# Mamba's drives: five of sixteen states formed by ScalarE with time on the partitions and turned into PSUM by TensorE

## What is computed

```python
xc = silu(conv(x @ W_in.T, W_conv) + b_conv)          # 256 channels
dt, B, C = split(xc @ W_x.T)                           # ranks 8, 16 and 16
dt = softplus(dt @ W_dt.T + b_dt)
A = -exp(A_log)
# for every time t, channel d, state n of 16:
h = h * exp(dt_t[:, :, None] * A) + (dt_t * xc_t)[:, :, None] * B_t[:, None, :]
y = einsum('bdn,bn->bd', h, C_t)
# y = (y + xc * D) * silu(z), then y @ W_out.T
```

## Time and profile before

| | us |
|---|---|
| median of 3 runs | 3919.7 (3919.11 to 3921.49) |
| the profiled execution, its span | 3921.5 |
| first scan of Mamba to the end of the last | 929.5 |
| from the start of the transformer to the end | 2899.6 |

### The profile page before, as it was taken

The page is one execution under the profiler, slowest core; times in us unless marked ns, Lnnn a source line. Parts: engine busy times, 40 slices in busy tenths (PEclk is TensorE's granted clock), DMA queues, the critical chain, the costliest instruction groups (busy, mean ns, idle before and its releaser), DMA issues.

```text
span 3921.5 us, 110568 instructions
## 1 busy us (share of the span) xinstructions
PE 3707.5 (95%) x43392; PEld 2518.5 (64%) x43392; DVE 3319.6 (85%) x3407; ACT 2915.4 (74%) x6890; POOL 3241.5 (83%) x2370
## 2 busy tenths in 40 slices
PE   7889989988789999999999999999999999999997
PEld 2333333333377777777777777777767777777775
DVE  4999999999688888888888887888878888788885
ACT  7555445553388887888888887888878888888885
POOL 3888888888698888888888888888888888888883
PEclk8999998998899999999999999999999999999999
DMA  1221222212100000000000000000000000000001
GB/s 68 73 76 70 76 71 75 76 71 83 50 16 2 16 3 2 17 2 16 3 6 13 2 16 2 6 13 3 16 2 6 13 2 16 2 6 2 2 3 44
DMA packets 31567, 102.12 MB, mean 26 GB/s; under 512 B 4676, under 2 KB 6600, under 8 KB 30928
## 3 DMA queue, kind: packets, MB, share of 16 engines
q1 hardware_dynamic: 31056, 95.05, 7.0%
HBM read 90.32 MB, written 4.72 MB: 24 GB/s over the span
## 4 chain that ended last, share of the span: by engine, by line
PE 68%; issue 2%; ACT 2%; DVE 0%; POOL 0%; POOLq 0%; ACTq 0%; DVEq 0%
PE ps L1116 17%; PE ps L1043 13%; PE ps L1105 9%; PE ps L1054 8%; PE ps L1093 7%; PE ps L1141 5%; PE ps L1154 3%; PE ps L1078 2%; PE ps L1065 1%; PE ps L1123 1%; PE ps L1129 1%; ACT prob L1246 0%; PE ps L1023 0%; ACT mixed L1255 0%; ACT w_qk L1175 0%
## 5 line engine op out<-in xcount | busy, mean ns | idle before, releaser
L1521 POOL TENSOR_TENSOR resid<-resid,sq 128x1024 f32<-128x1024 f32 x384 | 910.8, 2377 | 3.4 <-DVE sq L1376 2.9
L626 POOL TENSOR_TENSOR read<-state,c_row 128x1024 f32<-128x1024 f32 x256 | 719.8, 2831 | 153.9 <-DVE state L588 84.9
L1543 POOL TENSOR_TENSOR resid<-resid,rnorm 128x1024 f32<-128x1024 f32 x384 | 725.0, 1904 | 18.1 <-POOL rnorm L1535 0.4
L1116 PE MATMUL ps<-mixed,w_vo 128*128 128x128 f32 x6144 | 720.7, 276 | 3.0 <-ACT mixed L1255 2.8
L1116 PEld LDWEIGHTS ps<-mixed,w_vo 128*128 128x128 f32 x6144 | 711.5, 193 | 12.9 <-issue 4.6
L1043 PE MATMUL ps<-w_qk,xs_parts 128*128 128x512 f32 x2304 | 634.6, 411 | 35.4 <-issue 18.1
L1246 ACT ACTIVATE prob<-ps,stat 128x64 f32<-128x64 f32 x3072 | 653.5, 385 | 0.7 <-DVE stat L1396 0.5
L1376 DVE TENSOR_TENSOR sq<-ps,rope_l 128x1024 f32<-128x1024 f32 x384 | 462.4, 1204 | 101.5 <-ACT sq L1208 101.2
L393 PE MATMUL mamba_ps<-read,ident 128*128 128x512 f32 x1024 | 509.6, 638 | 15.4 <-POOL read L626 15.4
L1389 DVE TENSOR_TENSOR resid<-ps,rope_l 128x1024 f32<-128x1024 f32 x384 | 464.3, 1209 | 66.9 <-ACT sq L1208 59.7
L1043 PEld LDWEIGHTS ps<-w_qk,xs_parts 128*128 128x128 f32 x2304 | 412.4, 191 | 148.6 <-issue 73.8
(11 more groups left out here) (138 smaller groups left out, 5676.8 us busy)
## 6 DMA issues: line engine op xcount, KB each, us to landing
c_row<-c_rows SPq DMA_DIRECT2D x128, 512.0 KB, 3.6
w_stage<-w_qk_hbm SPq DMA_DIRECT2D x12, 512.0 KB, 4.7
vo_stage<-w_v_hbm SPq DMA_DIRECT2D x6, 512.0 KB, 3.7
vo_stage<-w_o_hbm SPq DMA_DIRECT2D x6, 512.0 KB, 4.6
xn<-x_hbm SPq DMA_DIRECT2D x4, 512.0 KB, 6.6
kept<-resid SPq DMA_DIRECT2D x8, 256.0 KB, 4.4
resid<-kept SPq DMA_DIRECT2D x8, 256.0 KB, 4.0
out_hbm<-resid SPq DMA_DIRECT2D x8, 256.0 KB, 2.0
```

What stands on the lines that cost most here:

```text
L626: pool.tensor_tensor(read[:, h, g % 2, :], state[:, h, g % 2, :], c_row[:, g % C_AHEAD, :], ALU.mult).then_inc(done[f"rd{h}"], 1)
L1116: last = pe.matmul(bank[:, 0:P], w_vo[:, l % 2, head_at(place_h), :], mixed[:, odd, place_h, :], start=place_h == 0, stop=place_h == HEADS ...
L1521: pool.tensor_tensor(qk[:, tile % 2, cols], qk[:, tile % 2, cols], sq[:, 1 + part, :], ALU.add).then_inc(done[f"rotated{part}"], 1)
L1543: pool.tensor_tensor(heads, heads, norms, ALU.mult).then_inc(done[f"normed{part}"], 1)
```

## The change

For the states 2, 5, 8, 11 and 14 the drive no longer comes from a spread row of B and VectorE. Once for each sequence TensorE turns `dtx` (16 transposes of 128x128, steps "tt0" to "tt3") and B (8 small ones, "tb"), and ScalarE copies them to `dtx_t` and `b_t`, which have time on the partitions. For each of the five states ScalarE scales `dtx_t` by the state's column of `b_t` (eight instructions of 128x256, "td", to `drive_t`), and TensorE turns the result back, eight transposes for each half, into a pair of banks ("p0", "p1"). The scan reads it from there. The step "b" and both drives of these states are gone. `DRIVE_IN_PSUM` shrinks from six states to three, so half 0's drive lies in SBUF for 8 states instead of 10. All order tables are new.

```diff
+DRIVE_IN_PSUM = (4, 10, 15)
+DRIVE_TURNED = (2, 5, 8, 11, 14)
+DRIVE_SPREAD = tuple(n for n in range(D_STATE) if n not in DRIVE_TURNED)
+TURNS_BY_STATE = 4
...
+        if name in ("b", "p0", "p1"):
+            pair = other
+            take(name, k, [2 * pair, 2 * pair + 1], (("sc1" if name == "b" else f"sc{name[1]}", k),))
+            if name == "b" and k % D_STATE in DRIVE_IN_PSUM:
+                take("dr0", k, [2 - 2 * pair, 3 - 2 * pair], (("sc0", k),))
...
+            if g % D_STATE in DRIVE_TURNED:
+                first = SLOTS[f"p{h}", g][0]
+                return ps[:, first:first + 2, :]
...
+                def turn_dtx(q):
+                    def stage(s):
+                        after(pe, ("tx0", s), ("tx1", s))
+                        to = free(f"tt{q}", s)
+                        for j in range(2):
+                            for h in range(HALVES):
+                                first = (2 * q + j) * P
+                                last = pe.transpose(to[:, (2 * j + h) * P:(2 * j + h + 1) * P], dtx[:, s % 2, h, first:first + P],
+                                                    ident[:, :])
...
+                def turn_drive(h):
+                    def stage(g):
+                        after(pe, ("td", g))
+                        free(f"p{h}", g)
+                        to = drive_of(h, g).rearrange("p c n -> p (c n)")
+                        for j in range(SEQ // P):
+                            last = pe.transpose(to[:, j * P:(j + 1) * P], drive_t[:, j, h * P:(h + 1) * P], ident[:, :])
...
+                def take_turned(q):
+                    def stage(s):
+                        after(act, (f"tt{q}", s), ("td", D_STATE * (s - 1) + LAST_TURNED))
+                        act.copy(dtx_t[:, 2 * q:2 * q + 2, :], bank(f"tt{q}", s).rearrange("p (j n) -> p j n", j=2)
...
+                def drive_turned(g):
+                    s, n = divmod(g, D_STATE)
+                    k = DRIVE_TURNED.index(n)
+                    before = D_STATE * s + DRIVE_TURNED[k - 1] if k else D_STATE * (s - 1) + LAST_TURNED
+                    after(act, *[(f"at{q}", s) for q in range(TURNS_BY_STATE)], ("ab", s), ("p0", before), ("p1", before))
+                    for j in range(SEQ // P):
+                        last = act.activation(drive_t[:, j, :], dtx_t[:, j, :], ACT.Identity, scale=b_t[:, s % 2, j, n:n + 1])
...
-                        after(dve, (f"dec{h}", g), (f"dr{h}", g), (f"rd{h}", g - 2))
+                        after(dve, (f"dec{h}", g), (f"p{h}" if g % D_STATE in DRIVE_TURNED else f"dr{h}", g), (f"rd{h}", g - 2))
...
-    nc = bacc.Bacc("TRN2", target_bir_lowering=False, num_devices=1)
+    nc = bacc.Bacc("TRN2", target_bir_lowering=False, num_devices=1, dynamic_dma_scratch_size=1024)
```

More of the change, by code:

```diff
@@ L128, in mamba_slots, with take @@
 def mamba_slots(pe):
-    single = {f"bc{c}": f"abc{c}" for c in range(2)} | {f"o{c}": f"ao{c}" for c in range(2)} | {
-        f"{a}{h}{c}": f"{b}{h}{c}" for a, b in (("x", "ax"), ("z", "az"), ("dt", "relu")) for h in range(HALVES) for c in range(2)}
-    slots, last, turn, pair = {}, [None] * 4, [0, 0], 1
-    def take(name, k, banks, reader):
-        slots[name, k] = banks[0], sorted({last[q] for q in banks if last[q]})
+    single = {f"bc{c}": (f"abc{c}",) for c in range(2)} | {f"o{c}": (f"ao{c}",) for c in range(2)} | {
+        f"{a}{h}{c}": b(h, c) for a, b in (("x", lambda h, c: (f"ax{h}{c}",)), ("z", lambda h, c: (f"az{h}{c}",)),
+                                           ("dt", lambda h, c: (f"abs{h}{c}", f"relu{h}{c}")))
+        for h in range(HALVES) for c in range(2)} | {f"tt{q}": (f"at{q}",) for q in range(TURNS_BY_STATE)} | {"tb": ("ab",)}
+    slots, last, turn, pair = {}, [()] * 4, [0, 0], 1
+    def take(name, k, banks, readers):
+        slots[name, k] = banks[0], sorted({x for q in banks for x in last[q]})
         for q in banks:
-            last[q] = reader
+            last[q] = readers
     for name, k in pe:
         other = 1 - pair
-        if name == "b":
-            pair = k % 2
-            take("b", k, [2 * pair, 2 * pair + 1], ("sc1", k))
-            if k % D_STATE in DRIVE_IN_PSUM:
-                take("dr0", k, [2 - 2 * pair, 3 - 2 * pair], ("sc0", k))
+        if name in ("b", "p0", "p1"):
[3 more added lines that the diff above has]
+                take("dr0", k, [2 - 2 * pair, 3 - 2 * pair], (("sc0", k),))
         elif name in single:
-            take(name, k, [2 * other + turn[other]], (single[name], k))
+            take(name, k, [2 * other + turn[other]], tuple((x, k) for x in single[name]))
             turn[other] ^= 1
@@ L167, in mamba @@
                 (MAMBA_PE, FRONT_PE), (MAMBA_ACT, FRONT_ACT), (MAMBA_DVE, FRONT_DVE), (MAMBA_POOL, FRONT_POOL), (MAMBA_SP, []))]
-        in_sbuf = [g for g in range(2 * BATCH * D_STATE) if g % D_STATE not in DRIVE_IN_PSUM]
+        in_sbuf = [g for g in range(2 * BATCH * D_STATE) if g % D_STATE not in DRIVE_IN_PSUM + DRIVE_TURNED]
         DRIVES, BEFORE = {g: i for i, g in enumerate(in_sbuf)}, dict(zip(in_sbuf[2:], in_sbuf))
@@ L373, in b_rows, with turn_b @@
                     last.then_inc(done["b"], 1)
+                def turn_dtx(q):
[7 more added lines that the diff above has]
+                                                    ident[:, :])
+                        last.then_inc(done[f"tt{q}"], 1)
+                    return stage
+                def turn_b(s):
+                    after(pe, ("abc0", s), ("abc1", s))
+                    to = free("tb", s)
+                    for j in range(SEQ // P):
+                        last = pe.transpose(to[:, j * D_STATE:(j + 1) * D_STATE], x_dbl[0:D_STATE, j * P:(j + 1) * P],
+                                            ident[0:D_STATE, 0:D_STATE])
+                    last.then_inc(done["tb"], 1)
+                def turn_drive(h):
[5 more added lines that the diff above has]
+                            last = pe.transpose(to[:, j * P:(j + 1) * P], drive_t[:, j, h * P:(h + 1) * P], ident[:, :])
+                        last.then_inc(done[f"p{h}"], 1)
+                    return stage
                 def add_skip(h):
@@ L408, in _ @@
                           "b": b_rows, **halved("sk", add_skip), **halved("y", add_read),
-                          **banked("o", output)}
+                          **banked("o", output), **{f"tt{q}": turn_dtx(q) for q in range(TURNS_BY_STATE)}, "tb": turn_b,
+                          **halved("p", turn_drive)}
                 for name, k in PE_SEQ:
@@ L484, in stage @@
                     def stage(s):
-                        after(act, (f"bc{c}", s), ("split", s - 1), ("cst", s - 1), *[(f"dt{h}{k}", s - 1) for h in range(HALVES) for k in range(2)])
+                        after(act, (f"bc{c}", s), ("split", s - 1), ("cst", s - 1), ("tb", s - 1), *[(f"dt{h}{k}", s - 1) for h in range(HALVES) for k in range(2)])
                         act.copy(x_dbl[:, cols(c)], bank(f"bc{c}", s)[0:BC_ROWS + DT_RANK]).then_inc(done[f"abc{c}"], 1)
@@ L495, in stage @@
                         def stage(s):
-                            after(act, (f"dt{h}{c}", s), (f"tx{h}", s - 2), (f"dr{h}", D_STATE * (s - 1) - 1))
+                            after(act, (f"dt{h}{c}", s), (f"tx{h}", s - 2), (f"dr{h}", D_STATE * (s - 2) + LAST_SPREAD),
+                                  *[(f"tt{q}", s - 2) for q in range(TURNS_BY_STATE)])
                             act.activation(tile[:, s % 2, h, cols(c)], bank(f"dt{h}{c}", s), func,
@@ L514, in softplus_log, with take_b @@
                     return stage
+                def take_turned(q):
+                    def stage(s):
+                        after(act, (f"tt{q}", s), ("td", D_STATE * (s - 1) + LAST_TURNED))
+                        act.copy(dtx_t[:, 2 * q:2 * q + 2, :], bank(f"tt{q}", s).rearrange("p (j n) -> p j n", j=2)
+                                 ).then_inc(done[f"at{q}"], 1)
+                    return stage
+                def take_b(s):
+                    after(act, ("tb", s), ("td", D_STATE * (s - 2) + LAST_TURNED))
+                    act.copy(b_t[:, s % 2, :, :], bank("tb", s)[:, 0:SEQ // P * D_STATE].rearrange("p (j n) -> p j n", n=D_STATE)
+                             ).then_inc(done["ab"], 1)
+                def drive_turned(g):
[3 more added lines that the diff above has]
+                    after(act, *[(f"at{q}", s) for q in range(TURNS_BY_STATE)], ("ab", s), ("p0", before), ("p1", before))
+                    for j in range(SEQ // P):
+                        last = act.activation(drive_t[:, j, :], dtx_t[:, j, :], ACT.Identity, scale=b_t[:, s % 2, j, n:n + 1])
+                    last.then_inc(done["td"], 1)
                 def decays(h):
@@ L529, in _ @@
                           **parts("relu", take_dt("relu", ACT.Relu, dtx)), **halved("ex", softplus_exp),
-                          **halved("ln", softplus_log), **halved("dec", decays)}
+                          **halved("ln", softplus_log), **halved("dec", decays),
```

(5 more changed lines are left out.)

63 lines of the change are left out of this document (31 added, 32 removed), and 101 rows, old and new, of tables (FRONT_ACT, FRONT_DVE, MAMBA_ACT, MAMBA_DVE).

## The result

The changed kernel takes 3941.0 us (median of 4 runs, 3938.33 to 3944.3), the kernel before 3919.4 beside it. The ratio is 1.0052, with a 95% interval of 1.0039 to 1.0064: half a per cent slower, where 3865 us were forecast. The profiled execution has a span of 3942.5 us.

| us | before | forecast | after | miss |
|---|---|---|---|---|
| start to the first scan | 80.7 | 83.7 | 92.2 | 8.5 |
| first scan to the end of the last | 929.5 | 871.8 | 902.2 | 30.4 |
| end of the last scan to the transformer | 11.7 | 11.7 | 14.3 | 2.6 |
| transformer | 2899.6 | 2899.6 | 2933.8 | 34.2 |

A forecast was written before the change was run, and what follows sets the result against it. The bound was to move from VectorE to TensorE, 106.9 + 3.0 = 109.9 us a sequence. 7 x (117.0 - 109.9) = 49.7, plus 8 for the last, less 3, gave 54.7 us off: 3865 us, range 3836 to 3911.

The forecast's parts named there:

- I leave the transformer at its time.: Transformer, after Mamba: the diff only merges semaphores that count the same instructions there, so it stays at 2899.6 us.
- within 5 us: Transformer: sign that the prediction is right, its time staying this close to 2899.6 us.
- VectorE's 111.8 - 12.0 = 99.8 us: VectorE in one Mamba sequence: busy 111.8 us, loses ten drives of 1.2 us, scans unchanged.
- The rival with half a GpSimd instruction ahead of each excluded one: VectorE in Mamba: 9 x 1.18 = 10.6 us of waiting a sequence, 3906 us in all; chance 0.13.
- the exclusion wholly on GpSimd's side, 104.0 us: GpSimd in one sequence: 84.6 of instructions, 8 x 2.27 for scans from SBUF, 1.2 for the split of B and C.
- The last sequence: Mamba's end: prepares no next sequence, so VectorE stays the bound; 8 of its 12.0 us counted as gain.
- TensorE's 106.9 us and 3.0 of waits: TensorE in one sequence: load of 106.9 us passes VectorE's; with waits taken as 3.0, 109.9 us.
- the two rivals on the clock: TensorE in Mamba: clock stays 0.93, 3921 us, chance 0.05; or transposes let it fall, 3956 us, chance 0.05.
- scalings of 0.50 us (0.32 to 0.61 expected): ScalarE in one sequence: 40 scalings, 17 us taken, and 3 us of copies; busy 78 to 90 of about 110, hidden.
- The front, "3 later": Before the first scan: ScalarE stands for the weights from 8.1, fewer waits later; first scan 3 us after 80.7.

## Why the prediction was wrong

**"I leave the transformer at its time."** This is the step that failed most: 34.2 of the 75.7 us, and the sign with it. The prediction looked for changed instructions in the transformer and found none that do other work. It did not ask what 1601 more instructions on the same engine move behind them. No rival had it, and "within 5 us" was the test that it failed. What the runs showed in its place is that where this code lies in the packets of 256 instructions makes all of it: 0, 65, 112 and 256 places gave 2899.6, 2934 to 2940, 2943.8 and 2899.6.

**VectorE's 111.8 - 12.0 = 99.8 us.** This step failed too, and it has most of the 30.4 us that Mamba misses by: with short reads of GpSimd 29 of them go. The twelve microseconds did go (176 drives instead of 256), but 9.4 came back as waiting for GpSimd. The rival with half a GpSimd instruction ahead of each excluded one is what happened: 1.04 us each measured, where it took 1.18; VectorE at 110.6 us, where it had 110.4; a period of 113.4, where it had 114.9. Its premise was only half right: the SBUF half comes first in four of eight states, and two of the other four wait as well. The sum had put the exclusion wholly on GpSimd's side, 104.0 us, since that was the side which paid before. That rival alone would have given 3906; with the 34.2 us of the transformer and the 8.5 of the front it comes to 3949, near the measured 3941.

**The last sequence** was to give 8 us and gave 1.4: it took 108.8 us instead of 102.2, which is 6.6 of Mamba's 30.4. With two scans in the other order it took 102.0, so this is most likely the same waiting; no run tries it by itself.

**TensorE's 106.9 us and 3.0 of waits** were near in their sum: 110.8 us a sequence once nothing else bounds it. The starts of the matmuls in that run give some 106.4 of load and 4.3 of waits, as an estimate that takes what a start lies more than 0.48 us behind the last as a wait. The clock was right: it rose to 0.96, and neither of the two rivals on the clock came about; the 96 transposes a sequence did not let it fall.

**ScalarE** was costed well: scalings of 0.50 us (0.32 to 0.61 expected), 398.3 / 5 = 79.7 us busy, hidden.

**The front, "3 later".** The wait was seen and its length known, from 8.1 to 17.4 at the latest, and then netted against fewer waits later. It stood on the chain: the first scan came 11.5 us later, and 7.6 of them go when the entry moves. The term was mis-sized by its own main part: 3 forecast, 11.5 measured.

**The end of Mamba** grew by 2.6 us, from the last scan to the transformer's first matmul. This was not tried.

## What to carry to other kernels

Code that is not touched is still moved: where an engine sends out hundreds of short instructions at a stretch, count its instructions ahead of that stretch modulo 256, and try two or three fillers before a change elsewhere is judged by the whole time. Where two engines exclude each other, removing work from one doesn't remove the exclusion; ask which of the two will start first in the new order, and whether that one or the other has time to give. And a wait for data put early into an in-order engine's queue counts in full, unless the row shows that the engine would have waited there anyway.

## What the runs showed of the hardware

- TensorE waits for its own instructions. 256 of them in one burst take 1.48 us. Stalls of up to 2.2 us inside such bursts end at one place of the packet, 195 or 196 by the count used here, in all eleven traces (118 stalls over 0.4 us), 1.2 to 1.6 us after a packet of 256 has landed, which itself takes 0.9 to 1.6 us.
- Waits that are already fulfilled show no cost on TensorE in Mamba that is clear of its spread: with 191 of them, 51 ns each in the trace, it takes 902.1 and 904.2 us, against 902.2 and 902.7 without and 909.1 with 47.
- A scan with both inputs in SBUF that meets a read of GpSimd lasts up to 4.47 us instead of 2.27, and which of the two waits mostly repeats from sequence to sequence: the scan of state 7 took 4.45 to 4.47 us in all eight.
